# Causal attention: PSUM slots from a ring of seven banks, with the transposed maxima in the same ring

## The reference, cut to what matters

```python
qkv = x @ Wqkv + bqkv
q, k, v = split into 16 heads of 8
att = jnp.einsum('bhqd,bhkd->bhqk', q, k) * scale
att = jnp.where(causal, att, -inf)
att = jax.nn.softmax(att, axis=-1)
y = jnp.einsum('bhqk,bhkd->bhqd', att, v)
y = y.transpose(0, 2, 1, 3).reshape(b, t, c)
return y @ Wproj + bproj
```

## Time and profile before

| what | value |
|---|---|
| three runs | 1084.04, 1086.39, 1088.76 us |
| the profiled execution: its time | 1078.19 us |
| its span, first to last instruction | 1076.5 us |
| mean granted TensorE clock | 0.855 of full speed |
| first maxima matmul of the causal stage | 701.49 us |
| last exponential starts | 938.8 us |
| causal stage ends | about 961 us |

### The profile page before, as it was taken

One profiled execution on the slowest core, in us unless ns is written; L12 is line 12 of the kernel. 1 busy time (PEld: TensorE's weight loads), 2 busy tenths in 40 slices (PEclk: granted clock), 3 DMA queues, 4 the chain that ended last, 5 costly groups with the idle time before them and its releaser, 6 DMA issues. The chain is left out here.

```text
span 1076.5 us, 15238 instructions
## 1 busy us (share of the span) xinstructions
PE 736.8 (68%) x5421; PEld 493.0 (46%) x5421; DVE 716.9 (67%) x1203; ACT 340.5 (32%) x579; POOL 411.6 (38%) x593
## 2 busy tenths in 40 slices
PE   0575145877775999836658792468787777738794
PEld 0354121477665998614455461233333333236462
DVE  7996484689996888389934234578887888244232
ACT  0211064000001550011211250417666666702152
POOL 3353100278886960034424254022333322302343
PEclk9987586689998999858958895759999999976897
DMA  7000000000000000030000212757100000000303
GB/s 180 0 1 1 11 0 0 1 1 1 2 1 1 2 2 1 15 117 1 1 0 31 79 41 73 244 97 114 28 8 9 8 9 8 7 3 13 89 32 106
DMA packets 42881, 35.89 MB, mean 33 GB/s; under 512 B 6167, under 2 KB 37336, under 8 KB 42808
## 3 DMA queue, kind: packets, MB, share of 16 engines
q1 hardware_dynamic: 40248, 29.61, 11.6%
q0 software_dynamic: 2560, 5.31, 1.5%
HBM read 17.45 MB, written 15.89 MB: 31 GB/s over the span
## 5 line engine op out<-in xcount | busy, mean ns | idle before, releaser
L1881 DVE TENSOR_REDUCE blockmax<-c_bank 128x8 f32<-128x1024 f32 x144 | 175.0, 1223 | 47.7 <-PE c_bank L2007 41.4
L1944 ACT ACTIVATE PT<-c_bank 128x1024 f32<-128x1024 f32 x144 | 145.5, 1025 | 71.8 <-PE c_bank L2029 71.7
L2043 PE MATMUL c_bank<-PT,V 128*9 128x256 f32 (+3 forms) x960 | 78.7, 431 | 14.5 <-POOL PT L1833 10.5
L798 PE MATMUL sums<-prod,ident 128*128 128x128 f32 x512 | 69.0, 293 | 27.0 <-DVE prod L824 27.0
L2000 PE MATMUL c_bank<-KA,QA 48*128 48x128 bf16 (+3 forms) x608 | 59.9, 282 | 36.0 <-DMA KA<-qk_parts_dram 16.2
L1833 POOL TENSOR_SCALAR_AFFINE_SELECT PT<-PT 128x256 f32<-128x256 f32 x128 | 49.1, 408 | 81.1 <-ACT PT L1944 81.0
L798 PEld LDWEIGHTS sums<-prod,ident 128*128 128x128 f32 x512 | 63.7, 203 | 32.2 <-DVE prod L824 32.2
L1539 POOL DMA_INDIRECT routed_results<-results_m,rows_m x48 | 46.0, 957 | 66.6 <-DVE results_m L1516 64.8
L2029 PE MATMUL c_bank<-QA,KA 51*128 51x128 bf16 (+3 forms) x480 | 56.8, 302 | 17.0 <-DMA QA<-nrows 16.5
L368 PE MATMUL gu_f<-gu_wT,xqT_f 128*128 128x352 f32 x128 | 52.8, 567 | 17.9 <-DVE h_f L298 17.9
L1522 DVE TENSOR_TENSOR r_h_m<-r_silu_m,r_gu_m 128x256 f32<-128x256 f32 x48 | 20.2, 421 | 66.9 <-ACT r_silu_m L1507 66.9
(11 more groups left out here) (320 smaller groups left out, 1801.8 us busy)
## 6 DMA issues: line engine op xcount, KB each, us to landing
sorted_rows<-blank SPq DMA_DIRECT2D x2, 1584.0 KB, 14.0
rows_m<-sorted_rows SPq DMA_DIRECT2D x12, 264.0 KB, 4.7
qk_parts_dram<-qk_parts SPq DMA_DIRECT2D x8, 384.0 KB, 3.4
QA<-qk_parts_dram SPq DMA_DIRECT2D x6, 384.0 KB, 8.0
KA<-qk_parts_dram SPq DMA_DIRECT2D x6, 384.0 KB, 9.7
back_m<-routed_results SPq DMA_DIRECT2D x8, 256.0 KB, 3.7
qk_parts_dram<-qk_parts SPq DMA_DIRECT2D x8, 256.0 KB, 3.2
m_gu<-in_rt_gate SPq DMA_DIRECT2D x1, 1024.0 KB, 6.0
```

What stands on the lines that cost most here:

```text
L798: ins = nc.tensor.matmul(sums[:, kind, 0], k.ident[:, :], prod[:, kind, e // HALF, :, e % HALF, :], start=(e == 0), stop=(e == DH - 1))
L1881: nc.vector.tensor_reduce(blockmax[:, h % 2, :, HALFQ * n:HALFQ * (n + 1)], slot_of((1, m)).rearrange("p b (n c) -> p b n c", c=P), AX.X, ...
L1944: nc.scalar.activation(PT[:, u % PRING, :, :], slot_of((0, u)), ACT.Exp, scale=SCALE).then_inc(s_pt, 1)
L2043: ins = nc.tensor.matmul(O[32 * g:32 * g + DH + 1, f * P:f * P + n], V[:, b, j, h, :], PT[:, u % PRING, b, o:o + n], start=(j == 0), stop= ...
```

## The change: how banks are handed out

The three slots of two banks become a ring of seven single banks. `ring_table` now walks through all items in PE's order, the transposes included, and gives each maxima or score item the next two banks and each transpose the next one, modulo seven. For every bank it notes who had it last; from these it keeps, for each kind (scores, maxima, transposes), the highest number that has to be finished, and `free_slot` waits for every kind in that list. `O` moves from bank 6 to bank 7; `tm` has no bank of its own any more.

When an item's two banks are 6 and 0 they are not neighbours. Its consumer is then issued as two instructions of 512 elements, one per bank (`halves_of`), and only the second counts the semaphore up. By the table this is so for 20 of the 144 score items and 20 of the 144 maxima items. What each item waits for, by the two tables: in the new one the newest item waited for is item n - 3 among scores and maxima, as before; 219 of the 288 items (104 scores, 115 maxima) now have a wait for a second kind beside it.

```diff
--- before.py
+++ after.py
@@ -1580,7 +1580,7 @@
 BEHIND = 2
 MASKS = [[k for k, (j, par) in enumerate(item) if PLACE[j] % 2 == par] for item in ITEMS]
 NMASK = sum(map(bool, MASKS))
-SLOTS_ST = 3
+RING_BANKS = (0, 1, 2, 3, 4, 5, 6)
 PRING = 6
 GROUPS = ((0, 1), (1, 2), (2, 4), (4, 8), (8, 12), (12, 16))
 EARLY = 3
@@ -1634,15 +1634,30 @@
 
 def ring_table():
 
-    order, m = [], 0
+
+
+    order, m, rows = [], 0, 0
     for u in range(-1, HEADS * NST):
         if u >= 0:
             order.append((0, u))
         while m < maxima_due(u):
             order.append((1, m))
             m += 1
-    place = {x: n for n, x in enumerate(order)}
-    return {x: (n % SLOTS_ST, order[n - SLOTS_ST] if n >= SLOTS_ST else None) for x, n in place.items()}
+        while rows < rows_due(u):
+            order.append((2, rows))
+            rows += 1
+    table, last, n = {}, {}, 0
+    for x in order:
+        mine = [RING_BANKS[(n + i) % len(RING_BANKS)] for i in range(1 if x[0] == 2 else BATCH)]
+        n += len(mine)
+        freed = {}
+        for at in mine:
+            if at in last:
+                kind, number = last[at]
+                freed[kind] = max(freed.get(kind, 0), number + 1)
+            last[at] = x
+        table[x] = (sorted(mine), sorted(freed.items()))
+    return table
 
 
 def causal_attention(k, w, parts_dram, tag="_c"):
@@ -1685,7 +1700,7 @@
         rec = k.sb("c_rec", [P, 2 * P], ctx=ctx)
         bank = k.ps("c_bank", [P, 8, BANK], ctx=ctx)
         ln = Norm(k, tag, ctx)
-        O, tm = bank[:, 6, :], bank[:, 7, :].bitcast(BF16)
+        O = bank[:, 7, :]
         (s_w, s_ldve, s_t, s_xT, s_qk, s_hi, s_rest, s_mid, s_lo, s_v, s_vcopy, s_set, s_fill, s_bias, s_ones, s_fresh) = (
             k.sem(n) for n in ("s_cw", "s_cldve", "s_ct", "s_cxT", "s_qk", "s_hi", "s_rest", "s_mid", "s_lo", "s_v",
                                "s_vcopy", "s_cset", "s_cfill", "s_cbias", "s_cones", "s_cfresh"))
@@ -1698,15 +1713,24 @@
         s_yt = [k.sem("s_yt0"), k.sem("s_yt1")]
         NOUT = 8
 
+        def halves_of(x):
+
+            low, high = ring[x][0]
+            return [slice(0, BATCH)] if high == low + 1 else [slice(b, b + 1) for b in range(BATCH)]
+
         def slot_of(x):
 
-            return bank[:, 2 * ring[x][0]:2 * ring[x][0] + 2, :]
+            low, high = ring[x][0]
+            return bank[:, low:high + 1:high - low, :]
+
+        def rows_of(h):
+
+            return bank[0:BATCH * PARTS * QT, ring[(2, h)][0][0], :].bitcast(BF16)[:, 0:P]
 
         def free_slot(eng, x):
 
-            before = ring[x][1]
-            if before is not None:
-                eng.wait_ge((s_pt, s_nm)[before[0]], before[1] + 1)
+            for kind, number in ring[x][1]:
+                eng.wait_ge((s_pt, s_nm, s_tme)[kind], number)
 
         with nc.Block() as block:
             @block.sync
@@ -1878,8 +1902,10 @@
                     if n == 0:
                         wait(dve, s_neg, h - 1)
                     dve.wait_ge(s_mx, m + 1)
-                    nc.vector.tensor_reduce(blockmax[:, h % 2, :, HALFQ * n:HALFQ * (n + 1)],
-                                            slot_of((1, m)).rearrange("p b (n c) -> p b n c", c=P), AX.X, ALU.max, negate=True).then_inc(s_nm, 1)
+                    for b in halves_of((1, m)):
+                        ins = nc.vector.tensor_reduce(blockmax[:, h % 2, b, HALFQ * n:HALFQ * (n + 1)],
+                                                      slot_of((1, m))[:, b].rearrange("p b (n c) -> p b n c", c=P), AX.X, ALU.max, negate=True)
+                    ins.then_inc(s_nm, 1)
                     if n == NMX - 1:
                         dve.wait_ge(s_nm, m + 1)
                         wait(dve, s_ms, h - 1)
@@ -1928,7 +1954,7 @@
                 def rows_out(h):
                     act.wait_ge(s_tm, h + 1)
                     wait(act, s_row, 16 * BATCH * h)
-                    nc.scalar.copy(nrows[:, :], tm[0:BATCH * PARTS * QT, 0:P]).then_inc(s_tme, 1)
+                    nc.scalar.copy(nrows[:, :], rows_of(h)).then_inc(s_tme, 1)
 
                 def copy_out(h):
                     act.wait_ge(s_av, (h + 1) * len(VALUES))
@@ -1941,7 +1967,9 @@
                         act.wait_ge(s_st, u + 1)
                         if u >= PRING:
                             act.wait_ge(s_av, group_with(u - PRING) + 1)
-                        nc.scalar.activation(PT[:, u % PRING, :, :], slot_of((0, u)), ACT.Exp, scale=SCALE).then_inc(s_pt, 1)
+                        for b in halves_of((0, u)):
+                            ins = nc.scalar.activation(PT[:, u % PRING, b, :], slot_of((0, u))[:, b], ACT.Exp, scale=SCALE)
+                        ins.then_inc(s_pt, 1)
                     while rows < rows_due(u):
                         rows_out(rows)
                         rows += 1
@@ -2010,8 +2038,8 @@
 
                 def max_to_rows(h):
                     pe.wait_ge(s_ms, h + 1)
-                    wait(pe, s_tme, h)
-                    nc.tensor.transpose(tm[0:BATCH * PARTS * QT, 0:P], nparts[:, h % 2].rearrange("p b s i -> p (b s i)"),
+                    free_slot(pe, (2, h))
+                    nc.tensor.transpose(rows_of(h), nparts[:, h % 2].rearrange("p b s i -> p (b s i)"),
                                         shifted[:, 0, :]).then_inc(s_tm, 1)
 
                 def score_item(u):
```

## The result

The changed kernel takes 1092.14 us (median of 13 runs, 1089.44 to 1096.67), the one before 1085.54 (13 runs beside it): ratio 1.006, 95% interval 1.0042 to 1.0078. It is 6.6 us slower where 1.6 was forecast; the time lies in the stated range, 1082 to 1096.5.

What follows compares the result with a forecast made beforehand. The prediction took no engine as full and the heads as paced by hand-overs between engines; 0.3 (exponentials) + 0.3 (reductions) + 1.0 (second waits) = 1.6 us on 1086.39 gave 1088.0 us, range 1082 to 1096.5.

Steps and rivals of the forecast that it cites:

- fully exposed halves: Rival: all 40 cut exponentials and reductions delay their successors, 6.0 us, 1093.4 with the second waits' 1.0; chance 0.10.
- a second wait that delays PE everywhere: Rival: an extra step ahead of the first weight load in all 219 items, 13 us, 1100.0 in full; chance 0.10.
- the prediction's own classes: Faster 0.07, same 0.73, slower 0.20, with about 0.5% (5.4 us) as what a measurement can tell from no change.
- The ring gets no deeper: Score and maxima slots: with seven banks item n still overlaps item n-3 and waits for its consumer; gain zero.
- Transposes in the ring, 0: Transposed maxima sharing the ring's banks: 1.45 us of cover before the bank's next use; cost 0, at most 4 us.
- Halves, 0.6 us: 20 exponentials and 20 reductions cut in two: 0.3 us each, upper ends 2.8 and 3.2 us.
- Second waits, 1.0 us: PE's score items: 17 late releases by a reduction, now the second wait, at 0.06 us each; other items 0.
- 14.0 to 14.1: Sign of being right: us per head in the changed kernel, against 13.98 before.
- the 14.8 that the prediction named as a sign of being wrong: Heads of 14.8 us or more would point to 13 us of second-wait delay over 16 heads.

Runs made afterwards that it cites:

- one wait: The changed kernel without each score and maxima item's wait for the older kind, leaving only that for item n - 3; ratio 1.0007 to the kernel before.
- two waits alone: The kernel before, with its three slots and no halves, given the changed kernel's waits in each score and maxima item; ratio 1.0043.
- the pad of 37: The kernel before with 37 more PE instructions that only wait, for a condition long met, ahead of the first maxima item; ratio 1.0004.
- halves alone: The kernel before with the same 20 exponentials and 20 reductions cut into two instructions of 512 elements, slots and waits as before; ratio 1.0001.
- second waits late: The kernel before with the changed kernel's second waits only from step 36 on, 141 of the 191 extra PE instructions; ratio 0.9983.
- the early ones: The kernel before with the changed kernel's second waits only in steps 0 to 26 (heads 0 to 2), 37 extra PE instructions; ratio 1.0038.
- a row of 219: The changed kernel with 219 more waiting PE instructions, for a condition long met, ahead of the first maxima item; ratio 1.0081 to the kernel before.

## Why the prediction was right in its range and wrong in its size

The range held, but in part by luck. It had been stretched up to 1096.5 for two rivals, fully exposed halves and a second wait that delays PE everywhere; neither came true, and the 6.6 us that fill it have another cause. Put into the prediction's own classes, a change of 0.6% is over its bound of 0.5% and counts as slower, which it gave 0.20, against 0.73 for the same.

- **The ring gets no deeper**: right. A maxima item waits for an exponential 60 times, 32.3 us, against 59 times and 31.7 before, and one wait per item gives the time of before.
- **Transposes in the ring, 0**: right; no wait for their copy appears.
- **Halves, 0.6 us**: right within what can be measured (1.0001, interval up to 1.0016, or 1.7 us).
- **Second waits, 1.0 us**: the step that failed, and in it one sentence: "For the other items the second wait is met long before; cost 0" took waiting time as an instruction's only price. As a term the second waits measured about 5 us (two waits alone 1.0043; changed against one wait 1.006 against 1.0007). The part that was priced came out as priced: in 16 score items the first weight load starts 0.12 us after the reduction that frees the slot, in the changed kernel and with two waits alone, against 0.05 before, together 1.1 us. The rest is the price of PE's longer program: its blocks come at other moments, and one then lands behind the last gather. The rival "the second wait delays PE everywhere" was near in asking whether the instruction feed is ahead of the matmuls, but it had a price spread over 219 items, and waits from step 36 on cost nothing.
- The cover that I did not name: the instruction supply beside three gathers in 30 us. The row that would have told is the "instruction" line of the DMA view. Before, two blocks got through in that stretch.

The heads show both: 14.02 us in the steady part, as forecast (14.0 to 14.1), and two of 19.1 and 15.1, beyond the 14.8 that the prediction named as a sign of being wrong.

Shown: the second waits of heads 0 to 2 cause the loss, the gathers' timing is needed for it, and the stop is at an instruction packet that lands late. Open in part: why 37 instructions ahead of the first maxima item are harmless and 37 spread over heads 0 to 2 are not. The packets show where the two part. The block beside the gather of heads 8 to 11 starts 8.3 us after that gather's first DMA with the pad of 37 (7.4 to 8.9 in the kernel before, one wait, halves alone and second waits late), and the next block slips through at 747.24, 0.5 us ahead of the last gather's first DMA. In the changed kernel the first of these blocks starts 10.9 us after the gather (11.1 with two waits alone, 9.5 with the early ones), and the next only behind the last gather. By these times a block that is late beside one gather pushes the next one into the following gather. Why the first is later by these 1 to 3 us is not shown.

No version here is faster than the kernel before.

## What to carry to other kernels

A wait that is long met still takes its place in the engine's instruction stream (0.11 us each in a row of 219 here) and makes the program longer; on an engine with thousands of short instructions look at the instruction packets of the DMA view, above all where a large transfer runs beside it. Leave out waits that an earlier wait of the same engine implies, and keep large transfers apart. Before expecting depth from a finer ring, count banks: with items of two banks, seven banks hold the same three items as six.

## What the runs showed of the hardware that I had not expected

A 16 KB instruction packet can land after a gather that fills the DMA engines for 10 us, with no packet of its queue in between for 12 us (746 to 758). PE then stopped for 2.15 us, and the lower clock level behind it cost about another 2 us, an estimate from the matmuls' 0.61 against 0.39 us. Stops of 0.33 and 0.88 us in two other kernels left the granted clock at 1.00.

PE has only about one block of its program in hand when the next one is fetched: of 638 blocks of 256 instructions the packet of a typical one starts 245 rows ahead of the edge at which PE would stand, and in all four stops PE stood at exactly that edge, 256 n + 449 rows, until 1.5 to 1.8 us after the packet's end.

A weight load behind two waits, the later of them the second, started 0.12 us after the reduction that released it, against 0.05 with one wait (16 score items each). Waits that are met start 0.11 us apart on PE.
